# Spiral-convolution block with a mixture of experts on one core: place's products behind the second group of down products

## What is computed

```
# x: (8, 1024, 128); LN(x) = (x - mean) / sqrt(var + 1e-5)
h  = LN(x)
a  = LN(h) * gamma + beta
x1 = conv(a) + h                      # complex decay filter along the 1024 tokens
m  = silu((LN(x1) * gamma + beta) @ w1 + b1) @ w2 + b2
x2 = x + m + x1
t  = LN(x2)
top2 = top_k(t @ router.T, 2);  p = softmax(top2 logits)
out = x2 + sum over the two chosen experts e of
      p_e * (gelu_exact(t @ w1_e.T + b1_e) @ w2_e.T + b2_e)
```

## Time and profile before

| | us |
|---|---|
| median of 3 runs | 461.05 |
| lowest and highest run | 461.0, 462.15 |
| profiled execution, time | 459.66 |
| profiled execution, span | 457.9 |
| PE busy in the span | 373.0 (81%) |
| DVE busy | 348.0 (76%) |
| ACT busy | 322.0 (70%) |
| POOL busy | 273.3 (60%) |

### The profile page before, as it was taken

The page is one execution under the profiler, slowest core; times in us unless marked ns, Lnnn a source line. Parts: engine busy times, 40 slices in busy tenths (PEclk is TensorE's granted clock), DMA queues, the critical chain, the costliest instruction groups (busy, mean ns, idle before and its releaser), DMA issues. The chain is left out here.

```text
span 457.9 us, 11199 instructions
## 1 busy us (share of the span) xinstructions
PE 373.0 (81%) x2716; PEld 318.6 (70%) x2716; DVE 348.0 (76%) x1320; ACT 322.0 (70%) x772; POOL 273.3 (60%) x339
## 2 busy tenths in 40 slices
PE   1275189988898979796994588999999999999970
PEld 1132147575766757475764588999999999999970
DVE  7999999969999998975248158776777677777770
ACT  4783389988888888866461555777777777777740
POOL 6980756665788898666446505675555555555551
PEclk9995589999999999999998579999999999999995
DMA  7649122020222222223202133454333333333200
GB/s 254 168 142 328 62 47 47 7 41 13 59 74 59 87 46 100 58 87 68 78 30 101 67 99 102 140 147 122 110 96 97 102 100 100 111 105 102 76 3 0
DMA packets 34434, 41.60 MB, mean 91 GB/s; under 512 B 5382, under 2 KB 29459, under 8 KB 34244
## 3 DMA queue, kind: packets, MB, share of 16 engines
q1 hardware_dynamic: 27236, 23.56, 17.9%
q0 software_dynamic: 7136, 17.33, 13.1%
HBM read 19.52 MB, written 18.92 MB: 84 GB/s over the span
## 5 line engine op out<-in xcount | busy, mean ns | idle before, releaser
L597 POOL DMA_INDIRECT out<-result,out_id x91 | 89.2, 980 | 89.7 <-DVE result L1476 70.6
L560 POOL DMA_INDIRECT sorted_rows<-rows,pos x64 | 71.5, 1117 | 32.2 <-issue 21.4
L999 PE MATMUL up_p<-xt,work 128*128 128x128 f32 x488 | 66.5, 281 | 0.0
L786 ACT ACTIVATE work<-mw_c 128x256 f32 x182 | 65.6, 414 | 0.3 <-issue 0.2
L835 PE MATMUL down_p<-w_sb,work 128*128 128x128 f32 x512 | 64.0, 279 | 0.0
L824 PE MATMUL up_p<-h_t,work 128*128 128x512 f32 x128 | 61.5, 610 | 2.9 <-ACT work L622 1.7
L835 PEld LDWEIGHTS down_p<-w_sb,work 128*128 128x128 f32 x512 | 59.7, 192 | 4.8 <-issue 4.8
L999 PEld LDWEIGHTS up_p<-xt,work 128*128 128x128 f32 x488 | 61.1, 197 | 0.2
L771 ACT ACTIVATE hid_t<-up_p 128x512 f32<-128x512 f32 x61 | 36.4, 597 | 30.4 <-PE up_p L999 30.3
L622 ACT ACTIVATE work<-up_p,b_all 128x512 f32<-128x512 f32 x64 | 42.4, 681 | 14.4 <-PE up_p L824 13.4
L812 PEld LDWEIGHTS turn_p<-ident,work 128*128 128x128 f32 x192 | 24.0, 152 | 36.9 <-ACT work L648 12.7
(11 more groups left out here) (236 smaller groups left out, 812.8 us busy)
## 6 DMA issues: line engine op xcount, KB each, us to landing
tin<-sorted_rows SPq DMA_DIRECT2D x91, 136.0 KB, 2.2
resid<-in_x SPq DMA_DIRECT2D x8, 512.0 KB, 3.9
resid<-work POOLq DMA_DIRECT2D x8, 512.0 KB, 4.6
sorted_rows<-zeros SPq DMA_DIRECT2D x29, 136.0 KB, 2.4
out<-result,out_id POOLq DMA_INDIRECT x91
work<-in_mw SPq DMA_DIRECT2D x1, 1024.0 KB, 6.5
sorted_rows<-rows,pos POOLq DMA_INDIRECT x64, 2.5
work<-in_w SPq DMA_DIRECT2D x1, 256.0 KB
```

The costliest lines, as they stand in the source:

```text
L560: g.indirect_dma_start(sorted_dram, bass.IndirectOffsetOnAxis(pos[b % 2][:, j:j + 1], 0), rows[b % ROWBUFS][:, j, :], None).then_inc(s_sor ...
L597: g.indirect_dma_start(out_rows, bass.IndirectOffsetOnAxis(out_id[k][:, :], 0), result[k][:, :], None, bounds_check=TOKENS - 1, oob_is_err ...
L786: last = s_.activation(ring[s % RING][:, k * EF:(k + 1) * EF], mw1_c[:, bass.ds(at[k], EF)], ACT.Copy)
L999: last = t.matmul(mid_p[s % DEEP][:, c * TILE:(c + 1) * TILE], ring[s % RING][:, c * 128:(c + 1) * 128], xt[s % DEEP][:, :], start=True, s ...
```

## The change

In iterations where both groups exist, the call of `place(chosen_b)` stands behind `mlp_down(i, 1)` and not in front of it. Batch i-2 exists from iteration 2 on and the loop ends with iteration 6, so five iterations are touched. The last batch, iteration 7, is written out apart and is not changed. No instruction is added or taken away, and each keeps what it waits for; the programs of the other four engines are the same.

```diff
                 if live(i):
                     mlp_down(i, 0)
                     mlp_up(i, 2)
+                if live(i):
+                    mlp_down(i, 1)
                 if live(chosen_b):
                     place(chosen_b)
-                if live(i):
-                    mlp_down(i, 1)
                 if live(b0):
                     xm_turn(b0)
```

## The result

| | before | after |
|---|---|---|
| median, us | 461.02 (4 runs, 459.81 to 462.15) | 471.67 (4 runs, 469.67 to 474.31) |
| ratio, 95% interval | | 1.0235 [1.0204, 1.0266] |
| profiled execution, time | 459.66 | 470.54 |
| profiled execution, span | 457.9 | 468.8 |

The change makes the kernel 10.7 us slower, 2.3%. The direction was forecast, the size was not: 465.0 with a range of 460.8 to 468.3 stood against 471.67. Ratios leave out one disturbed run of a later kernel (`only2`, 674.57 us at a mean clock of 0.565).

The account below looks back on a forecast made before the run. It took a ring of PE, DVE, POOL and ACT as the bound. Work and waits gave 0, clock falls 2.3 x 1.95 = 4.5, less 0.5, +4.0: 461.05 + 4.0 = 465.05, rounded 465.0 us, range 460.8 to 468.3.

Parts of the forecast that it names:

- The bound, and the move by work and waits: First part, iterations 2 to 6: ACT's rows end the stall at xm_turn; moving place behind the down group sums to 0.
- Rival B: Iterations 4 and 5: the later place is the cost, at most 2 x 0.5 = 1.0 us, 462.1; chance 0.05.
- The stalls: In front of xm_turn, iterations 2 to 6: two stalls become one of their sum, 2.55 to 3.3 us.
- That the clock falls in them: Joined stalls of iterations 2 to 6: TensorE falls from 2.4 to 1.2 GHz after 2.4 to 2.5 us; chance 0.68.
- Rival A: Joined stalls of iterations 2 to 6: the clock stays up, nothing happens, 461.05, at most 0.4 either side; chance 0.22.
- The number of falls: Iterations 2 to 6: one chance in three for three shorter stalls, two in three for two longer ones, 2.3 falls.
- The price of a fall: From xm_turn on: PE's work takes twice as long for 3.7 to 4.1 us, half of it lost, 1.95 each.
- The 0.5 taken off for slack: 0.3 us of PE's slack in two waits before conv_turn and some 0.2 that POOL may hide, off the falls' 4.5.
- Independence: Falls in iterations 2 to 6 priced as a number times one price, 2.3 x 1.95 = 4.5 us.
- Rival C: Stall of 2.43 in iteration 6: timed runs have clock falls there; filling it saves 1.0 us, 460.0; chance 0.05.

Follow-up runs that it names:

- only2: The kernel before with the new order in iteration 2 alone: 463.05 us, ratio to before 1.0034.
- fill14: The changed kernel with 14 identity products, read by nobody, behind place in each of the five iterations: 460.76 us, ratio to before 0.9992.
- pair45: The kernel before with the new order in iterations 4 and 5 only: 464.88 us, ratio to before 1.0093.
- fill5: The changed kernel with 5 identity products, read by nobody, behind place in each of the five iterations: 463.69 us, ratio to before 1.006.

## Why the prediction was right in its direction and wrong in its size

- **The bound, and the move by work and waits: right.** ACT ended the stall in front of `xm_turn` in each iteration before and after, `place` moved under the cover of the rotations, and DVE waits for `place` no more than it did. With the standstill filled, the new order costs 0.9992 of before. Rival B had no part in it.
- **The stalls: mostly right.** Told 2.9, 2.55, 2.55, 3.3 and 3.2; measured 3.24, 2.94, 3.18, 3.18 and 3.21. Where two stalls become one, some 0.4 comes on top of their sum: 3.24 against 1.55 + 1.31 in iteration 2, 2.94 against 1.31 + 1.24 in 3, and where 4 or 5 is changed alone, 2.92 against 2.55 and 3.71 against 3.31. The step had no such term. The 3.18 of iteration 5 stands behind an iteration with a fall.
- **That the clock falls in them: right**, shown by `fill14` and by the profiles. Rival A is out.
- **The number of falls: the step that failed first.** It gave each of the three shorter stalls one chance in three and each of the two longer ones two in three, because a stall of 2.43 had kept its clock. One profile is one draw: in other executions falls came behind stalls of 2.45, 1.91 and 1.58. Nor does a fall come only while PE stands; in `pair45` it came 1.3 us after PE had begun again (195.4 against 194.09). Told 2.3, found four and five; over all profiles 29 of 32 such stalls had one.
- **The price of a fall: too low, the second step that failed.** It took 3.7 to 4.1 us of dense work at the lower level from two places at which the clock rose, and so half of that, 1.95, for every fall. The short falls cost 1.6 in the profile after (1.1 to 1.7 in the others). Those that begin ahead of `xm_turn` have 5.4 to 5.8 us of dense work in them: the iterations lost 2.2 and 2.8, and 3.2 to the end behind the last, of which some 0.4 is more than half of the work and isn't explained. The sum that fits the first profile is 1.6 + 2.2 + 2.8 + 3.2 = 9.8, or 2.45 per fall, with 1.0 from ahead of the change. The 0.5 taken off for slack is seen once: in the iteration that lost 2.2, half of the work at the lower level is 2.7.
- **Independence: an assumption that held only in part.** A number times one price took falls as separate and equal. Behind an iteration with a fall, 16 of 19 falls were long; behind one without, 3 of 10. After a long fall, the next joined stall had a long fall in ten of ten cases, with 26.7 to 27.3 us from one `xm_turn` to the next. But a long fall also came with none ahead of it, and filling iteration 4 alone gave back 1.3 us and not 4.5 to 7. So the chain as the experiments had foretold it is not what makes the loss, and why the clock goes down ahead of `xm_turn` in one iteration and behind its start in another is not shown by any run.
- **Rival C: half right in its premise.** Timed runs of before do have falls, but taking the 2.43 stall away gained nothing that can be measured (0.9998, within 0.9 us to either side, where it told 1.0).

The Trainium skill, page "TensorE: Matmul & The Clock Gate", section "Terms", prices throttled time at roughly that time times (1 - K/N). For stretches of 6.8 us that would be an estimate of 3.4; the iterations lost 2.2 to 2.8, since PE stood still in the first 1.0 to 1.3 us of each. The trace agrees for the part in which PE has work. The same page of the Trainium skill, section "A second HAM failure mode: psum-queue depth-cycling", says of another kernel that short idles between groups of products can make the clock swing; the falls in `fill5` (behind 1.91) and in the old order's iteration 1 (behind 2.45) agree with it more than the prediction, which read one clean profile, allowed. That joining the stalls could then gain, as rival C had it, did not come true.

## What to carry to other kernels

Two waits of an engine with work between them are not worth the same as one wait of their sum when the engine is TensorE: joining them cost 2.3% here, though by waits alone nothing would have ended later. A second stall behind the first can pay for what a fall of the clock costs; a joined one has none behind it. Before work is moved between two stalls of TensorE, look at what length of standstill the move leaves and what stands behind it, and read the clock of more than one execution, since one profile without a fall does not show that a stall is safe. Where a stall can't be avoided, put real work or even products that nobody reads in it, and count what the real work's old place was covering.

## What the runs showed of the hardware

- The clock stayed at 1.2 GHz for 3.4 us where it fell after PE had begun to work again, and for 6.8 us where it had fallen 1.0 to 1.3 us ahead of that, in all nine such stretches of the two profiles of the changed kernel. In the other runs with joined stalls the bounds are the same: 3.4 us where it fell less than 0.5 us ahead of the work or later, 6.8 us where it fell 0.9 to 2.1 us ahead.
- A fall of 3.4 us between the two stalls of the old order cost nothing (24.38 and 24.89 us against 24.38 and 24.90), one of 3.4 us behind `xm_turn` 1.1 to 1.7 us, one of 6.8 us with work behind it 2.2 to 2.9 us.
- Single executions of one kernel differ, and their mean clock with them: before from 458.87 to 462.8 with a mean clock of 0.940 down to 0.925, after from 469.67 to 475.05 with 0.916 down to 0.903.
- Fourteen needless f32 products per iteration, 3.4 us of TensorE each time, cost nothing that can be measured and gave back the whole loss (471.67 to 460.76).
